# One order for all engines, the scan's stores on ScalarE's queue, and the step weights held stationary

## The reference

```
x = x + L0(gn(x))   # per-sample mixed experts: conv 1x1 256->64, 3x3 64->64, 1x1 64->256, routed by sigmoid
x = x + L1(gn(x))   # in-projection to 3 x 256, depthwise conv, selective scan over 196 permuted tokens, out-projection
x = x + L2(gn(x))   # 1x1 256->64, offsets by 3x3, deformable 3x3 conv with bilinear weights, 1x1 64->256
x = x + L3(gn(x))   # (conv + 1)^2 three times, with batch norms
```

## Time and profile before

| | us |
|---|---|
| median of three runs | 1043.89 |
| lowest, highest | 1036.54, 1048.52 |
| profiled execution | 1048.19 |
| its span, first to last instruction | 1046.0 |
| TensorE busy in the span | 935.8 |
| VectorE, ScalarE, GpSimd busy | 731.9, 550.1, 362.4 |

### The profile page before, as it was taken

The page is one execution under the profiler, slowest core; times in us unless marked ns, Lnnn a source line. Parts: engine busy times, 40 slices in busy tenths (PEclk is TensorE's granted clock), DMA queues, the critical chain, the costliest instruction groups (busy, mean ns, idle before and its releaser), DMA issues.

```text
span 1046.0 us, 19785 instructions
## 1 busy us (share of the span) xinstructions
PE 935.8 (89%) x7460; PEld 635.9 (61%) x7460; DVE 731.9 (70%) x2047; ACT 550.1 (53%) x1155; POOL 362.4 (35%) x320
## 2 busy tenths in 40 slices
PE   3788988999999899999999999999999998887766
PEld 2555656666666566666666666666666665646454
DVE  2567377786878587878878687878787868756332
ACT  1143353756556474748475655657474747361412
POOL 3013433435251625344342525152524343342200
PEclk9889999999999999999999999999999999889998
DMA  9101153352626253544536262626353444426060
GB/s 220 37 8 44 40 141 121 85 177 75 184 75 178 70 169 108 145 128 116 161 94 188 76 190 72 182 79 168 96 164 113 128 130 118 147 64 189 15 207 16
DMA packets 116547, 123.33 MB, mean 118 GB/s; under 512 B 64802, under 2 KB 99750, under 8 KB 116454
## 3 DMA queue, kind: packets, MB, share of 16 engines
q1 hardware_dynamic: 107812, 105.45, 34.6%
q0 software_dynamic: 6144, 13.71, 4.6%
q10 hardware_dynamic: 2498, 2.91, 1.2%
HBM read 84.31 MB, written 37.73 MB: 117 GB/s over the span
## 4 chain that ended last, share of the span: by engine, by line
PE 30%; DVE 24%; issue 17%; POOL 13%; ACT 9%; DMA 5%; SPq 1%; ACTq 0%; POOLq 0%; DVEq 0%
PE ps L625 27%; DVE c_w L1301 4%; ACT y L986 3%; POOL rs L1215 3%; POOL b_ex L1215 3%; POOL b_cr L1215 2%; POOL b_yp L1263 2%; ACT L986 2%; POOL b_res L1215 2%; DVE y L1306 2%; DVE x L1309 2%; DVE st L1336 2%; DMA b_yp<-y_turned,b_to 2%; DVE b_xf L1309 1%; DVE y L1309 1%
## 5 line engine op out<-in xcount | busy, mean ns | idle before, releaser
L1263 POOL DMA_INDIRECT b_yp<-y_turned,b_to x64 | 90.3, 1411 | 271.5 <-DMA y_turned<-b_yt 256.9
L625 PE MATMUL ps<-y,inw 128*128 128x392 f32 x384 | 140.2, 509 | 1.3 <-DVE y L1306 1.3
L1215 POOL TENSOR_TENSOR rs<-ve,root 128x4 f32<-128x4 f32 x64 | 66.1, 1032 | 200.9 <-DVE ve L1305 200.4
L1336 DVE BATCH_NORM_STATS2 st<-x 128x6 f32<-128x196 f32 x256 | 73.7, 350 | 88.0 <-POOL x L1215 76.0
L1301 DVE TENSOR_TENSOR c_w<-c_w,c_hat 126x1176 f32<-126x1176 f32 (+1 forms) x64 | 97.8, 1580 | 11.2 <-DMA c_w<-hat_turned 11.2
L625 PE MATMUL ps<-c_w,c_zt 126*64 126x196 f32 x896 | 88.7, 345 | 11.6 <-DVE c_w L1301 6.9
L625 PEld LDWEIGHTS ps<-y,inw 128*128 128x128 f32 x384 | 70.6, 194 | 46.4 <-issue 6.8
L625 PE MATMUL ps<-w,a_S 128*32 128x384 f32 (+2 forms) x1280 | 81.6, 392 | 7.5 <-DVE a_S L1309 5.7
L625 PE MATMUL ps<-c 128*128 128x256 f32 (+1 forms) x284 | 86.7, 442 | 0.0
L986 ACT ACT_TABLE_LOAD x50 | 64.2, 1283 | 37.5 <-PE ps L625 36.7
L625 PEld LDWEIGHTS ps<-c_w,c_zt 126*64 126x64 f32 x896 | 63.8, 142 | 31.8 <-issue 14.3
(11 more groups left out here) (203 smaller groups left out, 2025.3 us busy)
## 6 DMA issues: line engine op xcount, KB each, us to landing
c_w<-hat_turned SPq DMA_DIRECT2D x32, 771.8 KB
c_w<-hat_turned SPq DMA_DIRECT2D x32, 578.8 KB
z_turned<-c_z SPq DMA_DIRECT2D x32, 441.0 KB
c_zt<-z_turned SPq DMA_DIRECT2D x16, 882.0 KB
b_xp<-x_turned SPq DMA_DIRECT2D x32, 222.0 KB
x<-in_x SPq DMA_DIRECT2D x32, 196.0 KB, 2.7
y_turned<-b_yt SPq DMA_DIRECT2D x32, 196.0 KB
out<-x SPq DMA_DIRECT2D x32, 196.0 KB, 7.3
```

Source lines behind the costliest of these rows:

```text
L625: return nc.tensor.matmul(o, l, r, start=start, stop=stop)
L1215: return nc.gpsimd.tensor_tensor(out=o, in0=x, in1=y, op=op)
L1263: nc.gpsimd.indirect_dma_start(out=YP[:, m, h].rearrange("p b d -> p (b d)"), out_offset=None, in_=y_dram[g % 2], in_offset=bass.IndirectO ...
L1336: last = nc.vector.bn_stats(st[s][:, 2 * c + b, :], x[:, c, b, :])
```

## The change

1. **ScalarE's queue.** tb step 22 (two DMAs `y_turned<-b_yt` per group) moves from SP to ScalarE, directly behind ScalarE's own copy of yt half 0. It waits for VectorE's copy of half 1 there.
2. **Step weights stationary.** The projection becomes a tile `db` of its own: `mm(t[half(b), 0:N], dbcw[:, c, :], b_xf[:, c, b, :])`, four products of 196 columns with the weights (padded to 64 columns) stationary. ScalarE adds the bias while it copies to `b_row`; two transposes bring it to a tile `rows`, and VectorE copies that into `b_xt` (ta step 4). The two `xt` tiles hold four transposes each and are copied by one engine each. `b_xq` is now a view of `b_xp`; the addition of the bias and the table `b_bc` are gone. tb starts when the load of `b_xp` has landed.
3. **Order.** `PLAN` and `FROM` give way to `ORDER`, a string of stage letters per engine. The sequence repeats per group from about group 4 on.
4. **Banks.** The ring takes its bank from the table `BANKS`, one digit per take, instead of going round.
5. **Takes first.** A step now takes its bank before its other waits.
6. **Fillers.** `keep_busy` goes (three products of 392 columns a group). `take` now emits `BUSY` products of 128 columns with `group` as the stationary operand: 430 in all, seven in each group from 6 to 11 (three ahead of r1, four ahead of w1), more at both ends (73 with group 0, 72 with 14 and 106 with 15).

The order of TensorE in one period, from f2 step 1 of group g (stage.step, part left out; the group in brackets where it is not g): before f2.0 f2.1 n3.1(g-1) c0.13(g+2) f2.2 c0.1(g+3) f2.3 f2.5 x4 k3.1(g-1) f2.5 x4 n1.1 c0.2 k3.2 c0.4 tb.7 tb.10 x2 tb.11 x2 tb.12 c0.5 tb.12 s1.1 x2 tb.20 s1.1 k3.3 tb.21 x2 c0.6 x2 n0.1 s1.1 x3 c0.8 d2.2 ta.0 x2 o1.0 ta.0 o1.0 c0.10 d2.2 ta.0 o1.2 x2 d2.2 x5 n2.1 d2.4 c0.11. After: f2.1 c0.2(g+3) f2.2 c0.4 f2.3 tb.7(g+1) f2.5 x3 tb.10 x2 tb.11 x2 tb.12 x2 c0.5 f2.5 x3 tb.20 f2.5 x2 c0.6 x2 n1.1 n3.1(g-1) tb.21 x2 c0.8 s1.1 x6 c0.10 o1.0 d2.2 x2 k3.1 ta.0 x2 o1.0 ta.1 c0.11 ta.3 k3.2 o1.2 x2 c0.13 n0.1 k3.3 d2.2 x4 n2.1 d2.2 d2.4 c0.1.

On VectorE, the piece behind the scan's products, after: tb.19 x2, n3.1, n1.1, c0.7, f2.5 x2, d2.1, tb.21, s1.0, n3.3, d2.1, c0.9. And at the end of the period: c0.13 x2, n0.1, n2.0, c0.15, n2.1, tb.0, n2.3, c0.15, c0.0. On SP, after: f2.5 x2, d2.0 x2, f2.6 x2, d2.1, d2.2 x2, k3.5, ta.3 x2, n0.0; before: f2.5 x2, f2.6 x2, d2.0 x2, d2.1, d2.2, tb.22 x2, d2.2, k3.5, ta.3 x2, n0.0. GpSimd's four scatters (ta.2) now stand together, ahead of the two x adds (o1.3).

```diff
     def take(self, f, g):
-        self.turn[f, g] = len(self.turn)
+        bank = int(self.banks[len(self.turn)])
+        self.turn[f, g] = bank, self.uses[bank]
+        self.uses[bank] += 1
...
 def planned(name):
-    todo = []
-    for s, stage in enumerate(STAGES):
-        at = -1
-        for g in range(1 if stage == "once" else GROUPS):
-            for (i, part), start in zip(places(name, stage), PLAN[name][s], strict=True):
-                at = max(start + FROM[stage][g], at + 1)
-                todo.append((at, s, g, i, part))
-    return sorted(todo)
+    todo = {}
+    for letter, stage in zip(LETTERS, STAGES, strict=True):
+        todo[letter] = iter([(stage, g, i, part) for g in range(1 if stage == "once" else GROUPS)
+                             for i, part in places(name, stage)])
+    return [next(todo[letter]) for letter in ORDER[name]]
...
             def take(f, g, ring=R):
                 ring.take(f, g)
                 pe.wait_ge(ring.drained(f, g), ring.empty(f, g))
-                return ring.tile(f, g)
+                t = ring.tile(f, g)
+                for _ in range(BUSY.get((f, g), 0)):
+                    mm(t[:, 0:128], k128("group"), k128("group"))
+                return t
...
             def ta(i, part, g):
-                k, tt, b = part, part // G, part % G
...
-                for h in range(HEADS):
-                    nc.tensor.transpose(t[0:HT, h * XD:h * XD + HD], b_xf[:, h, b, cols], ident)
-                o = t[0:HT, 0:HEADS * XD].rearrange("p (h x) -> p h x", h=HEADS)[:, :, HD:XD]
-                for c in range(CC):
-                    last = mm(o, b_xf[:, c, b, cols], dbcw[:, c, :, :], start=(c == 0), stop=(c == CC - 1))
...
+                if i == 1:
+                    t = take("db", g)
+                    for c in range(CC):
+                        for b in range(G):
+                            last = mm(t[half(b), 0:N], dbcw[:, c, :], b_xf[:, c, b, :], start=(c == 0), stop=(c == CC - 1))
...
+                if i == 3:
+                    t = take("rows", g)
+                    drained(pe, "db", g)
+                    for tt in range(2):
+                        last = nc.tensor.transpose(t[0:HT, tt * 128:(tt + 1) * 128], b_row[:, tt * HT:(tt + 1) * HT], ident)
...
             def f2(i, part, g):
-                if i == 0:
-                    keep_busy("c1", g, 1)
...
-                if i == 2 and part == 0:
-                    keep_busy("off", g, 2)
...
+                if i == 22:
+                    m = part
+                    if m == 0 and g > 1:
+                        for h in range(HEADS):
+                            act.wait_ge(*y_back[h].at(g - 2))
+                    drained(act, ("yt", m), g)
+                    nc.scalar.dma_start(y_dram[g % 2].rearrange("(h t p) x -> t p h x", h=HEADS, t=2)[m],
+                                        YT[:, m].rearrange("p h b d -> p h (b d)")).then_inc(y_out.sem(g), 16)
```

More of the change, by code:

```diff
@@ L719, in c0 @@
                     b = part
+                    t = take(("w2", b), g)
                     if b == 0:
@@ L806, in tb @@
                     k = part
+                    t = take(("same", k), g)
                     if k == 0:
@@ L1234, in ta @@
                 if h == 0:
-                    for b in range(G):
-                        drained(pool, ("xt", 2 * m + b), g)
+                    drained(pool, ("xt", m), g)
+                    if m == 0:
+                        drained(pool, "rows", g)
                 nc.gpsimd.indirect_dma_start(
@@ L1452, in ta @@
                 if i == 0:
-                    k = 2 * part + 1
-                    if part == 0 and g:
+                    if g:
                         v.wait_ge(*x_out.at(g - 1))
-                    filled(v, ("xt", k), g)
-                    copy(XT[:, k // 2, :, k % 2, :], R.tile(("xt", k), g)[0:HT, 0:HEADS * XD]
-                         .rearrange("p (h x) -> p h x", h=HEADS)).then_inc(R.drained(("xt", k), g), 1)
+                    filled(v, ("xt", 1), g)
+                    copy(XT[:, 1, :, :, 0:HD].rearrange("p h b x -> p (h b) x"), R.tile(("xt", 1), g)[0:HT, :]
+                         .rearrange("p (q x) -> p q x", x=HD)).then_inc(R.drained(("xt", 1), g), 1)
                 if i == 4:
-                    if first(g):
-                        v.wait_ge(tables, 1)
-                    v.wait_ge(*x_back.at(g))
-                    tt(xq[:, :, :], XP[:, :, :, :, HD:XD].rearrange("p t h b x -> p (t h b) x"), b_bc[:, :, :], ALU.add)\
-                        .then_inc(b_xq_ok.sem, 1)
+                    filled(v, "rows", g)
+                    for tt in range(2):
+                        last = copy(XT[:, tt, :, :, HD:XD], R.tile("rows", g)[0:HT, tt * 128:(tt + 1) * 128]
+                                    .rearrange("p (b r) -> p b r", b=G)[:, :, 0:HEADS * DBC]
+                                    .rearrange("p b (h x) -> p h b x", h=HEADS))
+                    last.then_inc(R.drained("rows", g), 1)
             def tb(i, part, g):
@@ L1493, in tb @@
                     m = part
+                    if m == 0 and first(g):
+                        v.wait_ge(tables, 1)
                     ins = tt(MD[:, 4 * m:4 * m + 4, :].rearrange("p (h b) c -> p h b c", b=G),
```

327 lines of the change are left out of this document (137 added, 190 removed), and 23 rows, old and new, of tables (BUSY, PARTS).

## The result

| | before | changed |
|---|---|---|
| median of the runs, us | 1044.1 | 1087.76 (1085.62 to 1090.67) |
| ratio, 95% interval | | 1.043 [1.036, 1.049] |
| span of the profiled execution | 1046.0 | 1085.5 |
| c_off of groups 0, 3, 11, 15 | 139.7, 309.6, 761.7, 989.2 | 137.2, 318.5, 803.4, 1026.1 |
| mean period between groups 3 and 11 | 56.5 | 60.6 |

A forecast was written before the change was run, and what follows sets the result against it. TensorE was taken to bound the middle, one group's chain through all engines the ends. Start -4, 11 periods x -0.6, end -2 make -12.6 us on 1048.19: 1035.6, or 1031 on the medians' scale, range 1022 to 1038.

The forecast's parts named there:

- Work of TensorE: TensorE per period: old fillers out -2.3 us, new ones in +1.5, projection about even; net -0.8 us.
- even, a wait of some 0.4 at most: At pt: 10.8 us of TensorE work after yt covers y's 10.75 us trip from copy through store and gathers.
- rival B: Later z copies on VectorE make c_zt land late: 2.5 us late gives 1065, 1 us gives 1046; chance 0.20.
- The y stores on ScalarE costed at 0: Moving the y stores off SP saves 0.7 us of issue time there, but SP is not bound, so 0.
- n2's wait: On TensorE, norm product n2 waits 0.8 us for GpSimd's x2 add, which stands behind four scatters.
- r1's wait: On TensorE, r1 waits about 1.2 us behind its three fillers, as VectorE's b_cd waits for b_xp's load.
- off, 0.85 forecast: On TensorE, off waits 0.85 us for the c_pad writes on ScalarE.
- The sum of the hand layout: TensorE's period: about 4.3 us of waits over 51.4 + 0.1 of work and fillers, 55.9 us, no gain.
- -0.6: Gain taken per period, in us, between 0 layout and -0.8 by work alone; fillers called mostly covered.
- a drop more or fewer: One clock drop to the lower level more or fewer is worth 4 us, included in every range.
- The ends: Start -4 us (bounds -9 and +10), groups 11 to 15 -2 (bounds -8 and +6), last stage 0.
- "Slower" had 0.20: Whole kernel over 1% slower, above 1054.3 us, by late c_zt and a start losing 10 us; chance 0.20.

The follow-up runs named there:

- e9: All parts of the change in the old kernel's order, with banks in turn, fillers at the old places and y stores on SP: 1043.7 us, ratio 0.996.
- e2: The kernel before with only the y stores moved from SP to ScalarE: 1113.7 us, ratio 1.065.
- e5: e2 with SP made to wait for both b_yt copies before the second hat load: 1051.2 us, ratio 1.001 to the kernel before.
- e6: The changed kernel with SP's second hat loads and output stores held until the last gather landed, groups 2 to 11: 1089.6 us, ratio 1.043.
- e11: The changed kernel with VectorE's last two c_z copies ahead of n3's and n1's steps: 1098.2 us, ratio 1.049.
- e1: The changed kernel with the y stores back on SP: 1084.0 us, ratio 1.037.
- e10: The changed kernel with GpSimd's two x adds between the second and third scatter, groups 1 to 11: 1101.6 us, ratio 1.052.
- e12: The changed kernel with x adds between the scatters, c_z copies early, and the first pt behind two acc parts, d1 and xt: 1094.8 us, ratio 1.043.
- e16: e9 with b_cd ahead of gs on VectorE and b_ab ahead of y on ScalarE, groups 4 to 12: 1136.1 us, ratio 1.086.
- e17: The changed kernel with b_cd and b_ab behind a_md in groups 3 to 13, the first pt later, x adds between the scatters: 1046.6 us, ratio 1.002.
- e15: The changed kernel with b_cd and b_ab behind a_md in groups 4 to 11, the first pt later, x adds between the scatters: 1061.5 us, ratio 1.012.

## Why the prediction was wrong, point by point

- **Work of TensorE: right in kind.** -0.8 us a period forecast; 53.6 busy became 52.4, which is -1.2. The projection was forecast even, and e9 shows that the parts cost nothing.
- **The step that failed: "even, a wait of some 0.4 at most" for pt.** The trip copy, store, gathers was taken with the old durations, 10.75 us, to be covered by 10.8 us of TensorE's work. From the same copy (577.12) to pt (589.57) it now takes 12.45 us: 1.1 more until the first gather and 0.6 more from there to pt, where its DMAs meet the z store, the hats and the output. TensorE's work covered 10.5 of it, and 1.98 were left as the wait, 2.7 in the mean: the largest of all. That the company of other DMAs stretches such a trip is shown by e2 and e5. Here e6 shows it for the way from the first gather to pt, at least 2.7 us of which go with the hat loads and output stores; what makes the way to the first gather longer isn't shown (e11 made it longer still). I knew the burst (rival B) and priced it only for c_zt, where the trace has two waits of 5.3 us together in the whole run. The mechanism was at another address.
- **The y stores on ScalarE costed at 0: about right here (e1), for a wrong reason.** In the old order this edit alone costs 6.5% (e2), and the earlier trace rows gave the hint: I wrote that the hat load was "held up by them" and counted it as nothing. By the rule that I cited beside it, the Trainium skill (DMA: Bandwidth & Descriptors, Issuing engines are not separate DMA queues), only issue time is saved; the runs agree that ScalarE's queue itself is as good as SP's (e5, 1.001), and disagree that nothing else changes: what stood behind the moved DMAs goes out earlier.
- **n2's wait, 0.8 forecast, 1.3 measured.** The reason given (x adds behind four scatters) was the right place; the size was off, and ms took 1.42 us, 1.26 over its usual 0.16, with GpSimd's adds over it. With the adds earlier the wait was gone (e10). All durations of the layout were from an order in which the two engines met less.
- **r1's wait, 1.2 forecast, 0.4 measured.** b_cd's place ahead of gs was seen, and "lands at about the same moment" was right. What I missed is what such a place means: it has next to no slack, so it took back what the x adds gained (e10, e12), and it costs 92 us where the load is later (e16).
- **off, 0.85 forecast, 0.1 measured; c2, 0.4 and 0.4; yt, 0.6 and 0.** A wait for a_S, 0.55 measured, had no term.
- **The sum of the hand layout is wrong by its own terms.** It puts 4.3 us of waits on "51.4 + 0.1 of work and fillers" and gets 55.9. But the seven fillers are 1.5 us, and r1's 1.2 is said to be behind its fillers, so they don't lie in it. The busy 53.62 less 0.8, with 4.3 of waits, is 57.1, which is 1.3 more than before. Then -0.6 was taken because the fillers are "mostly covered", which had been counted already. The trace has the fillers in the 52.4 busy us, and 5.6 idle beside them. This alone turned a loss of 1.3 us a period into a forecast gain of 0.6.
- **No term for the clock.** Waits by hand were 4.3 us a period; the trace has 5.7. With that and 0.4 less work the 57.1 become 58.1, and 58.0 is the period at full clock. The 2.6 from there to 60.6 come mostly by the clock. I wrote that a drop more or fewer is worth 4 us and left it there; there were nine in eight periods, each beside a wait for b_yp (seven, of 2.1 to 5.4 us) or behind one for st (two, of 1.3), and none in e9.
- **The ends.** c_off of group 0 was forecast at 139.7 or a little before, and is at 137.2. The next three periods were to be 7 us of work shorter; TensorE was busy 160.2 us in them for 159.5, idle 21.1 for 10.4, and they were 11.4 longer. Waits for b_yp and c_zt and 17 us at the lower clock stand there (3.4 before), but e17, with the middle mended, is still 8.1 longer there, and no run tested the ramp by itself. The -2 between groups 11 and 15 was -4.8, and the last stage, forecast unchanged, was 2.6 longer. Rival B's 1065 and 1046 are on the profiled execution's scale, unlike the 1031 beside them.
- **The rivals.** "Slower" had 0.20, by c_zt, and the 1087.8 is above the whole range. Its indicator, an idle entry ended by b_yp of over 1 us in every period, was in the text and is what happened.

What stays open: e17's gain over the sum of its steps. Alone the three gave about -1.0, +1.0 and -1.2 hundredths of the ratio against the changed kernel's 1.043; together -4.1. e12 against e15 (1.043 and 1.012) suggests that b_cd's place is what lets the others count, but e12 also had the c_z copies moved, so the size of it isn't clean. A kernel with e9's middle and the new order's tail wasn't tried.

## What to carry to other kernels

When a DMA leaves a queue, cost what stood behind it in that queue, not only the DMA: it was a throttle for free, and one explicit wait puts it back. In an order by readiness, look for operations that wait for a round trip through DRAM and stand ahead of a short chain that TensorE needs; "ready just in time" is a place with little slack, and it can turn a mend elsewhere into a new wait. Mend such places together, and judge none of them by its run alone. When waits are laid out by hand, add the filler work once, either as work or as cover.

## What the runs showed of the hardware

- In the changed kernel TensorE waited 2.0 to 5.4 us for b_yp in each of eight periods, and in seven of them the lower clock level (1.2 GHz) set in during that wait or at most 1.3 us after it. With 3.4 or 6.8 us of it the period was 59.7 to 61.4 us for 58.0 at full clock. In e9, with 2.4 us idle a period and no listed wait over 0.6, the clock stayed at its full level.
- A VectorE operation on 128x4 took up to 1.42 us in the changed kernel, 9 times its usual 0.16, while GpSimd added; moving the adds made it 0.16 to 0.27 again (e10).
- Moving two stores of 196 KB to another issuing queue left their own trip as it was (2.3 us from the last issue to the first gather) where what they had held back was held by other means (e5), and made it 5.3 us where it wasn't (e2).
